# A transformer block with 16 routed experts: expert tiles of one 128-token list each in place of two 64-token lists, and the last pair of sequences with row buffers of its own

## The reference

```
h = layer_norm(word[x] + seg + posi + modal + npi + time2vec(delay) + time2vec(age))
h = h + attention(_layernorm(h))            # 12 heads of 16, q and k RMS-normed, per sequence of 128
x = _layernorm(h)
normed  = rms_norm(x) * ln_w
probs   = softmax(normed @ w_router)        # 16 experts
expert  = argmax(probs)                     # one expert per token
keep    = rank of the token within its (sequence, expert) <= 64
next    = relu(normed @ wi[expert]) @ wo[expert] if keep else normed      # 192 -> 768 -> 192
out     = h + x + max(probs) * next
```

## Time and profile before

| what | value |
|---|---|
| median of 3 runs | 405.36 us (401.0 to 406.44) |
| profiled execution | 408.49 us, of which its span is 406.8 us |
| PE busy | 320.6 us (79% of the span) |
| DVE, ACT, POOL busy | 262.2, 191.6, 203.8 us |
| mean granted TensorE clock | 0.913 of full speed |
| the chain that ended last | PE 58%, POOL 11%, ACT 10%, issue 8%, DVE 7%, DMA 3% |

### The profile page before, as it was taken

One profiled execution on the slowest core, in us unless ns is written; L12 is line 12 of the kernel. 1 busy time (PEld: TensorE's weight loads), 2 busy tenths in 40 slices (PEclk: granted clock), 3 DMA queues, 4 the chain that ended last, 5 costly groups with the idle time before them and its releaser, 6 DMA issues.

```text
span 406.8 us, 9205 instructions
## 1 busy us (share of the span) xinstructions
PE 320.6 (79%) x3246; PEld 234.4 (58%) x3246; DVE 262.2 (64%) x743; ACT 191.6 (47%) x405; POOL 203.8 (50%) x250
## 2 busy tenths in 40 slices
PE   0058798989889888998987803389999999999990
PEld 0056657769677676977867602345556666555560
DVE  7467846887878788767485636846656565556620
ACT  0613644967768687763844612033333333333320
POOL 5767650552553626401001446577666666755420
PEclk9999967998989899896998965599999999999997
DMA  5328820126152352703208951139311221111100
GB/s 138 89 63 222 244 60 1 21 60 176 33 161 72 96 146 48 203 1 99 75 9 246 291 154 39 39 105 293 107 46 51 60 58 54 48 46 53 48 3 0
DMA packets 33589, 38.22 MB, mean 94 GB/s; under 512 B 6480, under 2 KB 30777, under 8 KB 33556
## 3 DMA queue, kind: packets, MB, share of 16 engines
q1 hardware_dynamic: 25940, 24.58, 21.3%
q0 software_dynamic: 7040, 12.63, 12.5%
q10 hardware_dynamic: 576, 0.59, 0.4%
HBM read 31.36 MB, written 7.21 MB: 95 GB/s over the span
## 4 chain that ended last, share of the span: by engine, by line
PE 58%; POOL 11%; ACT 10%; issue 8%; DVE 7%; DMA 3%; POOLq 0%; ACTq 0%; SPq 0%; DVEq 0%
PE psum L1363 11%; PE psum L1140 7%; PE psum L1342 7%; PE psum L1141 7%; POOL weights L396 6%; PE psum L1347 4%; PE psum L1354 3%; PE psum L1258 3%; ACT shared L574 3%; PE psum L1175 3%; PE psum L1210 2%; POOL blk_token L458 2%; ACT L574 2%; PE psum L1134 2%; DMA token_rows<-shared 2%
## 5 line engine op out<-in xcount | busy, mean ns | idle before, releaser
L1087 DVE COPY shared<-weights 128x1152 f32 x96 | 69.1, 763 | 10.6 <-issue 10.5
L1258 PE MATMUL psum<-ident 128*128 128x128 f32 x200 | 34.0, 334 | 38.1 <-DMA qk_norm<-in_qk_norm 24.5
L473 POOL DMA_INDIRECT tower_out<-shared,oidx x24 | 37.1, 1547 | 38.6 <-DVE shared L1101 38.0
L1258 PEld LDWEIGHTS psum<-ident 128*128 128x128 f32 x200 | 32.6, 247 | 39.2 <-issue 24.5
L1363 PE MATMUL psum<-shared 128*64 128x192 f32 x576 | 52.1, 330 | 0.9 <-ACT shared L672 0.9
L404 POOL TENSOR_TENSOR small<-small,eps_of 128x2 f32<-128x2 f32 x32 | 6.8, 212 | 89.7 <-DVE small L768 66.2
L1363 PEld LDWEIGHTS psum<-shared 128*64 128x64 f32 x576 | 39.2, 137 | 19.4 <-issue 13.8
L1101 DVE SCALAR_TENSOR_TENSOR shared<-psum,shared 128x192 f32<-128x192 f32 x24 | 10.0, 418 | 46.0 <-PE psum L1363 46.0
L1140 PE MATMUL psum<-shared,weights 96*128 96x192 f32 (+1 forms) x96 | 36.2, 464 | 0.8 <-ACT weights L527 0.7
L1342 PE MATMUL psum<-shared 128*64 128x384 f32 x192 | 36.3, 499 | 0.5 <-ACT shared L664 0.5
L668 ACT ACTIVATE shared<-psum 128x768 f32<-128x768 f32 x24 | 19.5, 811 | 36.4 <-PE psum L1347 36.4
(11 more groups left out here) (179 smaller groups left out, 704.2 us busy)
## 6 DMA issues: line engine op xcount, KB each, us to landing
weights<-in_wo SPq DMA_DIRECT2D x16, 576.0 KB, 7.2
weights<-in_wi SPq DMA_DIRECT2D x32, 192.0 KB, 5.2
weights<-in_wi SPq DMA_DIRECT2D x32, 96.0 KB, 5.5
token_rows<-shared SPq DMA_DIRECT2D x14, 192.5 KB, 2.8
tower_out<-shared SPq DMA_DIRECT2D x14, 96.0 KB, 2.3
vectors<-in_vectors SPq DMA_DIRECT2D x1, 672.0 KB, 4.7
token_rows<-shared ACTq DMA_DIRECT2D x2, 192.5 KB, 2.8
blk_token<-expert_lists,blk_entry POOLq DMA_INDIRECT x24, 2.7
```

The costliest lines, as they stand in the source:

```text
L473: G.indirect_dma_start(out=out, out_offset=bass.IndirectOffsetOnAxis(ap=oidx[q % 2][:, :], axis=0), in_=res[q % 2], in_offset=None, bounds ...
L1087: V.tensor_copy(w_now[q % 2][k][:, lo:hi], weights[:, bass.ds(at[k] + lo, hi - lo)]).then_inc(sem(("wi_now", "wo_now")[part]), 1)
L1258: T.matmul(dst, ident[:, :], ident[:, 0:width], start=True, stop=True)
```

## The change

`BT` becomes 128: a tile is one list of one expert. The first 16 tiles are the first list of each expert, read with the weights where they lie; 15 further tiles (`NLATE`) are enough for any routing, and these alone are planned and have their weights copied. There are thus always 31 tiles. The lists come with one load of the whole table to SBUF (`list_sb`, by SP), from which the first 16 tiles' tokens are used directly and the others' copied by DVE (`take_tokens`); the 24 gathers of `list_tile` are gone. There are 6 row buffers, and 5 gathers run ahead. The last pair has its own `row_last` and `x2_last`, without waits on `out_plain`. `places(0)` moves ahead of the `turn_qk` and `guard_scores` of pair 7, POOL does 6 of the first 8 list stores ahead of the `power` of pair 7 and 2 behind it, the logits of pair 6 go to another PSUM bank, so that `attend(7, 0)` comes ahead of them, and `unrouted(7)` comes ahead of the plan.

```diff
-BT = P // 2
+BT = P
-NBLK = NSEQ * P // BT + NE
-NTILE = NBLK // 2
+NLATE = NSEQ * P // BT - 1
+NTILE = NE + NLATE
+NGROW = 6
...
         def final(i):
             return isinstance(i, int) and i == NPAIR - 1
         def row_of(i, u):
             return row_last[u] if final(i) else row[u]
         def x2_of(i, u):
             return x2_last[u] if final(i) else x2[u]
         def tokens_of(q):
             return list_sb[:, q:q + 1] if q < NE else blk_token[:, q - NE:q - NE + 1]
         def logit_ps(i, u):
             if isinstance(i, int) and i == NPAIR - 2:
                 return psum_s[0][:, u, 0:NE]
             return psum_m[u][:, LG:LG + NE]
...  SP
-            sp.wait_ge(sem("p_logit"), NSEQ)
+            sp.wait_ge(sem("listed"), 16 * NSEQ)
+            load("lists_read", list_sb, lists.rearrange("(p q) o -> p (q o)", p=P))
...  POOL
-                    enlist(0, 0, 8)
+                    enlist(0, 0, 6)
                 if live(i + 1):
                     power(i + 1, (MV3 + 1, RSTD3), 1, "mv3", "rstd3")
+                if isinstance(i, int) and i == NPAIR - 2:
+                    enlist(0, 6, 8)
...
-            list_tile(0)
-            list_tile(1)
             pool.wait_ge(sem("out_plain"), 32 * (NSEQ - 2))
             pool.wait_ge(sem("rows_last"), 32)
+            pool.wait_ge(sem("lists_read"), 16)
+            for q in range(NGROW - 1):
+                gather_rows(q)
...  ACT
-                    freed(act, sem("out_plain"), 64 * i)
-                    normalize(x2[u], h1[u], u, RSTD3, NMR3).then_inc(sem("x2"), 1)
+                    if not final(i):
+                        freed(act, sem("out_plain"), 64 * i)
+                    normalize(x2_of(i, u), h1[u], u, RSTD3, NMR3).then_inc(sem("x2"), 1)
...  DVE
+            def take_tokens(j):
+                dve.wait_ge(sem("lists_read"), 16)
+                col = dve.value_load(blk_list[0:1, j:j + 1], min_val=0, max_val=NLISTS - 1)
+                V.tensor_copy(blk_token[:, j:j + 1], list_sb[:, bass.ds(col, 1)]).then_inc(sem("blk_token"), 1)
+            def take_weights(q, part):
+                lo, hi = ((0, WI_COLS), (WI_COLS, WCOL))[part]
+                if q >= NE + 2:
+                    dve.wait_ge(sem(("b_hid", "b_y")[part]), q - 1)
+                V.tensor_copy(w_now[q % 2][:, lo:hi], weights[:, bass.ds(at + lo, hi - lo)])...
...  PE
             def attend(i, u):
-                freed(pe, sem("logits"), 2 * i + u - 1 if not isinstance(i, int) or i else 0)
+                if final(i):
+                    pe.wait_ge(sem("nT"), 2 * i + u - 1)
+                else:
+                    freed(pe, sem("logits"), 2 * i + u - 1 if not isinstance(i, int) or i else 0)
...
+            def w_of(q):
+                return w_by_expert[:, q, :] if q < NE else w_now[q % 2]
             def hidden(q):
+                w = w_of(q)
                 for b in range(2):
-                    for k in range(2):
-                        T.matmul(hid_ps[k * BT:(k + 1) * BT, b, :], gT[:, b * P + k * BT:b * P + (k + 1) * BT],
-                                 w_now[q % 2][k][:, b * WI2:(b + 1) * WI2], start=True, stop=False)
+                    T.matmul(hid_ps[:, b, :], gT[:, b * P:(b + 1) * P], w[:, b * WI2:(b + 1) * WI2], start=True, stop=False)
                 for b in range(2):
-                    for k in range(2):
-                        at = (1 - b) * P + k * BT
-                        last = T.matmul(hid_ps[k * BT:(k + 1) * BT, b, :], gT[REST[b], at:at + BT],
-                                        w_now[q % 2][k][REST[b], FF:WI_COLS], start=False, stop=True)
+                    last = T.matmul(hid_ps[:, b, :], gT[REST[b], (1 - b) * P:(2 - b) * P], w[REST[b], FF:WI_COLS],
+                                    start=False, stop=True)
             def output(q):
                 for c in range(FC):
-                    for k in range(2):
-                        last = T.matmul(psum[q % 2][k * BT:(k + 1) * BT, 3, 0:D], ...)
+                    last = T.matmul(psum[q % 2][:, 3, 0:D], hidT[:, c * P:(c + 1) * P],
+                                    w[:, WI_COLS + c * D:WI_COLS + (c + 1) * D], start=c == 0, stop=c == FC - 1)
```

More of the change, by code:

```diff
@@ L121, in tower_kernel @@
         wproj = share_a(2 * D)[0:HALF + 1, :].rearrange("p (k f) -> p k f", k=2)
-        w_now = [[share_b(WCOL) for _ in range(2)] for _ in range(2)]
-        share_a(4 * WCOL - 4992 - HEADS * HPAD)
+        w_now = [share_b(WCOL) for _ in range(2)]
+        grow_low = [share_b(ROW) for _ in range(2)]
+        share_b(2 * WCOL - 2 * ROW)
+        share_a(2)
+        row_last = [share_a(ROW) for _ in range(2)]
+        share_a(4 * WCOL - 5378 - 2 * ROW)
         row = [share_a(ROW) for _ in range(2)]
@@ L134, in tower_kernel @@
         gT = share_b(2 * P)
-        grow = [share_b(ROW) for _ in range(4)]
+        grow = [share_b(ROW) for _ in range(NGROW - 2)] + grow_low
         ident = sb("ident", [P, P])
@@ L225, in terms_of, with final, row_of, x2_of @@
             return terms_odd[u] if odd_start(i) else terms[u]
+        def final(i):
+            return isinstance(i, int) and i == NPAIR - 1
+        def row_of(i, u):
+            return row_last[u] if final(i) else row[u]
+        def x2_of(i, u):
+            return x2_last[u] if final(i) else x2[u]
         def terms_free(eng, i):
@@ L600, in turn_pair @@
                     whole_turns(i + 4, 0)
+                ending = isinstance(i, int) and i == NPAIR - 2
+                if ending:
+                    copy_pv(NPAIR - 1, 0)
                 if live(i):
@@ L608, in turn_pair @@
                     values(i + 2, 0)
-                if live(i):
+                if live(i) and not ending:
                     based(i)
@@ L617, in turn_pair @@
                     exp_logits(i)
+                if ending:
+                    based(i)
                 if live(i + 1):
@@ L879, in experts_in @@
                     dve.wait_ge(sem("rstdn"), i + 1)
-                    freed(dve, sem("out_plain"), 64 * i)
-                    V.scalar_tensor_tensor(row[u][:, 0:D], x2[u], cols(small[u], RSTDN, 1), lnw_bc,
+                    if not final(i):
+                        freed(dve, sem("out_plain"), 64 * i)
+                    V.scalar_tensor_tensor(row_of(i, u)[:, 0:D], x2_of(i, u), cols(small[u], RSTDN, 1), lnw_bc,
                                            ALU.mult, ALU.mult).then_inc(sem("normed"), 1)
@@ L1104, in _ @@
[L1104 to L1109 removed]
+            planned(V.tensor_tensor(big, total_over(expert_iota[:, :]), ej.unsqueeze(2).broadcast_to([P, NLATE, NE]), ALU.is_equal))
@@ L1293, in turn_pair @@
                         turn_x(i + 2, 1)
+                ending = isinstance(i, int) and i == NPAIR - 2
+                if ending:
+                    attend(NPAIR - 1, 0)
                 if live(i):
@@ L1303, in turn_pair @@
                 if live(i + 1):
-                    attend(i + 1, 0)
+                    if not ending:
+                        attend(i + 1, 0)
                     attend(i + 1, 1)
@@ L1316, in turn_pair @@
                         keep_busy(psum_s[0][:, 2, 0:P], P, FILL_B)
+                    if isinstance(i, int) and i == NPAIR - 3:
+                        places(0)
                     turn_qk(i + 2, 0)
```

205 lines of the change are left out of this document (96 added, 109 removed).

## The result

| | before | changed kernel |
|---|---|---|
| median | 403.92 us (401.0 to 406.44, 4 runs) | 432.94 us (427.6 to 435.13, 4 runs) |
| ratio | 1 | 1.061 (95%: 1.052 to 1.070) |
| profiled execution | 408.49 us, span 406.8 | 430.96 us, span 429.2 |

The changed kernel is slower by 6.1%; the forecast was 5.1%, 426 us, in a range of 417 to 438. The medians are over all runs; the ratio is over fast runs alone, which leaves out the two of the changed kernel that lie over 1.5% above its fastest (430.96 and 427.6 us remain). A second measurement on another chip gave 1.057 (1.048 to 1.066).

A forecast was written before the change was run, and what follows sets the result against it. PE was taken to bound phase B. Tile 0 at 257.1 us plus 170.6 for phase B gave a span of 427.7, 429.4 with 1.7 around it, against 408.49; on the median 426 us, range 417 to 438.

The forecast's parts named there:

- The period: PE's time per 128-token tile in phase B: steps sum to 5.13 us, 5.1 taken, against 5.37 before.
- The floor of 4.93: Lowest tile time in phase B by the profile's rows, 1.03 + 1.30 + 0.65 + 1.95 us.
- The overlap: Second half of `hidden`: two 64-row products run side by side, 0.75 us taken, bounds 0.65 and 1.30.
- The count: Phase B: 31 tiles in place of 24, 7 more periods of 5.1, 35.7 us more.
- The end: From the last `turn_rows` to the end of the span: 18.8 us, against 19.25 before.
- The start: Tile 0 of phase B starts at 257.1 us, 8.0 us earlier, bounds 255 to 261.
- The records: Rival 1, phase B: tile time goes by number of records, 3.2 us a tile, 370 us on the median; 4%.
- the serial rows: Rival 2, second half of `hidden`: 64-row products don't overlap, period 5.75, +20 us, 446 us; 7%.
- The tile gains nothing: Rival 3, phase B: surplus over streaming belongs to step handovers and stays, period 5.37, 434 us; 15%.
- The start is not earlier: Rival 4, before phase B: something replaces the removed waits, tile 0 at 263 to 265, 432 to 434 us; 12%.
- pair 7's guards gain 3 us: End of phase A: with `count(0)` moved ahead, guards start at about 216.9 us, gaining 3 us.
- the root of pair 7 is bound by POOL: End of phase A: `power(7)` waits behind POOL's list stores, not statistics; result at 233.4, 5.3 us less counted.

The follow-up runs named there:

- after_full_rest: Changed kernel with the second half of `hidden` made over all 128 rows, so no step has another shape; period 5.48 us, total not used.
- before_one_block: Kernel before with the products of block 1 of each tile left out; 402.28 us, tile 5.34 us.
- tail_again: Kernel before with all changes of the end of phase A, measured a second time; ratio 0.987, median 400.57 us.
- tail_alone: Kernel before with all changes of the end of phase A, first measurement; ratio 0.979, median 399.93 us.
- order_alone: Kernel before with `places(0)` earlier, split list stores and moved logits, pair 7 still in the common buffers; 399.81 us in one execution.
- blocks_alone: Changed kernel with the old end of phase A; ratio 1.082, 441.08 us.

## Why the prediction was right

The direction and its reason hold: PE bounds phase B, a full-width product costs what two half-width ones do side by side, and 7 more tiles outweigh everything that the earlier start gives. The total came 1.5 us from the span (427.7 forecast, 429.2 measured), but because errors cancelled: phase B was 6.0 us longer than forecast (176.6 against 170.6) and tile 0 4.5 us earlier. 3.2 of these 4.5 us are the early lead of that execution, which is luck. Over the runs, 1.061 of 405.36 is 430 us where 426 was forecast.

- **The period**, 5.13 by the sum and 5.1 taken, was 5.23. The steps were off in both directions. I had the transposes at 1.03 "the same eight", and they take 0.88: in `after_full_rest` too, so it is not the 64-row step that decides it. They took 1.02 to 1.03 in each profile in which the products beside them have 64 columns of stationary, also with half of these products left out (`before_one_block`), and 0.87 to 0.88 in each in which these have 128. So their surplus of 0.15 goes with the changes of shape ahead of them and behind them. I counted changes of shape in the steps of products alone. The three steps of products were each 0.07 to 0.10 longer than forecast. I had divided their surplus over streaming between the shapes and the handover by feel, 0.08, 0.10 and nothing where 0.15, 0.20 and 0.10 were measured; `after_full_rest` leaves 0.05 for the whole tile without changes of shape. The floor of 4.93 takes the two remaining changes as free, and they were not. The mis-sized term cost 28 x 0.13 = 3.7 us.
- **The overlap** of the 64-row products, which no row of before had, is as taken.
- **The count**: 37.8 us for 7 tiles, 35.7 forecast.
- **The end**: from the last `turn_rows` 20.9 us (429.2 - 408.34) in place of 18.8. Of the 2.1 us 1.8 lie after the last scatter (10.45 against 8.7), where I had expected no difference.
- **The start**: 8.0 us forecast, 12.5 measured. 3.2 of it is the early lead of that execution. The remaining 9.3 are 7.4 up to the last `slot_all` (6.7 forecast) and 1.9 behind it (1.3 forecast). Step by step on this way: the guards gained 3.1 us against pair 6's (21.8 us behind them, 25.0 before; 3 forecast). The list stores before the root were six, and ended at 228.5, so the root came at 229.6, 16.0 us behind the first guard of pair 7, against 18.7 before. That is near the 2.6 us forecast for two stores less (2 x 1.28), and the third norm followed it at once, where before it had come 2.3 us later. The table's load took 1.8 us (2.3 taken).
- **Rivals.** The records (4%) and the serial rows (7%) are ruled out by runs. "The tile gains nothing" (15%) was nearly as near as my own case: of the 0.27 us a tile that I counted on 0.14 came. (The 20 us that I put on the serial rows should have been 28 x 0.65 = 18.) "The start is not earlier" (12%) did not happen.

Two things in the working rested on no row. That pair 7's guards gain 3 us depends on PE's clock just ahead of them. The stretch from pair 6's guards to pair 7's was 21.8 us in the changed kernel, 23.5 when measured again, 21.8 in `tail_again` and 24.9 in `tail_alone`, where nothing was left of the 3 us. Busy time by stretch, first of the changed kernel in its first profile, then of it measured again, then of `tail_alone`, at PE's `project` of pair 6 and behind it (the granted clock is the third number from the end):

```profile
210.00:215.00 5.00, 4.96 (x74) 4.55 (x73) 3.93 (x13) 3.74 (x10) 0.88 (x2) 1.00 0.71 217
```

```profile
210.00:215.00 5.00, 4.96 (x51) 4.73 (x52) 3.07 (x13) 2.20 (x5) 0.88 (x2) 0.84 0.74 218
```

```profile
210.00:215.00 5.00, 4.03 (x17) 3.36 (x18) 4.04 (x16) 2.17 (x9) 0.00 (x0) 0.72 0.05 18
215.00:220.00 5.00, 5.00 (x28) 4.74 (x27) 3.07 (x13) 1.29 (x3) 0.88 (x2) 0.59 0.74 212
```

PE waits 1.3 us for ACT ahead of `project` in all of them, and whether the clock then falls from 2.4 to 1.2 GHz decides over up to 3 us. In the two profiles of the changed kernel `project` starts at the same moment (208.00 and 208.03), and the operands of pair 7's scores are transposed from 210.47 in the one and from 212.16 in the other (1.7 us), which is all of the difference at the guards. Why the clock fell in one and not in the other no row shows.

And that the root of pair 7 is bound by POOL and not by the statistics does not hold everywhere. It holds in before, `order_alone`, the two profiles of the changed kernel and the two of the end of phase A alone. In `blocks_alone` and `before_one_block` both came within 0.2 us of each other, in the latter the statistics last. In all six profiles taken beside a kernel before of over 428 us the statistics came 5 to 9 us after the last list store ahead of the root, so the number of these stores decided nothing there.

## What to carry to other kernels

When small products already fill the array side by side, making one large product of two gains only the shape changes between them (here 0.14 us of a tile of 5.37, two changes less of four); count the tiles first, since padding to larger tiles (31 x 128 rows in place of 24 x 128) is paid in full periods. Two changes bundled into one should be measured apart: here the small one is worth 1.3 to 2.1% by itself, hidden under a loss of 8%. An interval between two events of the same profile shows such a part better than totals, but only its pieces show what is steady (here 4 us) and what comes and goes with the clock (0 to 3 us). A new order on a queue pays nothing while another wait, here two common buffers, ends at the same place.

## What the runs showed of the hardware

A change of TensorE's shape between 128 x 128 and 64 x 128 cost 0.1 us of the neighbouring step (1.45 against 1.36, 2.05 against 1.95), and by estimate 0.2 us with its share of the 64-row step, with nothing of it visible as idle time of PE. Eight transposes took 0.88 us between products with 128 columns of stationary and 1.03 between products with 64. Leaving out one of two products that lay side by side in the array changed a tile from 5.37 to 5.34 us (column halves) and a step from 0.85 to 0.84 us (row halves). PE's granted clock in phase A differed between executions of the same code at the same place (1.00 and 0.84 from 210 to 215 us in two profiles of the changed kernel), and the time from the last scatter to the end of the span was 8.7, 9.25 and 10.45 us with 24 tiles of two lists, 24 of one and 31 of one, by a cause that no row names.
